# Expert weights of the first chunk: twelve of sixteen rows through DRAM instead of through the PE array, and the router of the other chunks at four steps a period

## The chip, the cores and the metric

The kernel runs on one core of one Trainium2 chip. The metric is the time of one execution on the device, in microseconds; lower is better. Before the change the median of three runs is 518.84 us (518.59 to 519.28).

## The reference, cut to what matters

The program is two layers of several sublayers with residual additions over an input of 16 x 128 tokens of width 128. The change touches only the last sublayer, a mixture of attention projections in which every token weighs 16 experts:

```python
logits = xn @ sn - jax.nn.sigmoid(gates)          # n = 2048 tokens, 16 experts
...
w = jax.nn.softmax(masked, axis=-1)               # the expert weights, (2048, 16)

def moe_proj(p):
    y = jnp.einsum('nc,ech->neh', x, p)
    return jnp.einsum('ne,neh->nh', w, y)
q = moe_proj(q_proj).reshape(b, t, -1)
k = moe_proj(k_proj).reshape(b, t, -1)
v = moe_proj(v_proj).reshape(b, t, -1)
...
o = jnp.einsum('bts,bsh->bth', attn, v).reshape(n, h)
z = jnp.einsum('ne,nh->enh', w, o)
out = jnp.einsum('enh,ehc->nc', z, o_proj)
```

## The kernel before, in words

Everything is written by hand: each of the five engines has its own function with its instructions in order, and semaphores join them. A signal's name stands for a stretch of one of these semaphores (table `LANES`), and `q.wait_ge(name, n)` waits for its n-th signal.

The 2048 tokens lie along the free dimension, in four chunks of 512. Tokens are columns, so weighing the tokens for an expert takes that expert's 512 weights in a row that is the same on all 128 partitions: a *row* of expert weights. The last stage is one loop over `STEPS` = 67 periods k, written in the same shape in `tensor`, `scalar` and `vector`. Period k works on product n = k for the vector and scalar engines and on product n = k - 3 (`LAG`) for the tensor engine; chunk c = n // 16, expert e1 = n % 16:

- VectorE computes `zf` = X5 times the row (L1591, called w(n) below), then the lower half of the split of the product before, l(n) (L1552, `lower`). Then come steps of other work.
- ScalarE rounds `zf` to fp16, the upper half `z_hi` (L988).
- TensorE multiplies both halves by the expert's q and k weights (L673, six matmuls of 512 columns) and its v weights (L681, twelve of 128 columns). This is product P(n). The sums over the experts stay in banks 0, 1 and 2 until P(15), P(31), ..., after which ScalarE (L1010, L1012) and VectorE (L1610) copy q, v and k out.

The buffers `zf` and `ZH` are rings of four, so w, z_hi and l run at most four products ahead of TensorE.

A row reaches all partitions in two ways. For chunk 0, `spread_weights(e1)` (L660) does it in TensorE: a matmul of 32 rows by 512 columns with a selection matrix, into bank 6 or 7. One spread stands in every period up to k = 14. For chunks 1 to 3 the weights are transposed (L733, twelve small transposes, in period `TURN` = 11), copied by ScalarE into 16 partitions (`WTS`, L994, in period `SEND` = 12), written to a DRAM tensor `wd` by one DMA (L1745), and read back by one DMA for each row, which repeats the row on 128 partitions (L1749, 256 KB each), into the places `WR[16]` to `WR[31]` for chunk 1. The vector engine waits for these rows in pairs.

The weights themselves come from the router: 35 dependent small VectorE instructions, once for chunk 0 (before the loop) and once for chunks 1 to 3 together. The latter (`others`) are put into the periods from k = 3 on, five to a period:

```python
if k >= 3:
    for _ in range(5):
        next(others, None)
```

The transposes of period 11 wait for the last of these steps.

Just ahead of the loop TensorE ends the stage before (`mlp_down`, L622), transposes the chunk 0 weights (L652, `turn0`), and ScalarE copies them (L967, `wt16`), adds the bias to the last part of X5 (L945) and squares it (L949); TensorE's logits of chunk 3 (L632, L635) wait for those.

Of the kernel before, what the change touches and what calls it, by code (L numbers as in the profile page):

```python
# [7 lines left out]
F32 = mybir.dt.float32  # L8
# [5 lines left out]
ALU = mybir.AluOpType  # L14
# [36 lines left out]
    (("down", 48), ("weffmm", 4), ("ret_amm", 1), ("fwt", 3), ("wbotmm", 8), ("zmm", 4), ("mlp_down", 16), ("prod_o", 48), ("tile", 4)),  # L51
    (("mean", 4), ("vvmm", 4), ("turn0", 1), ("qkvmm", 12)),
    (("varmm", 4), ("ppmm", 4), ("logits", 4), ("turnw", 3), ("scores", 4)),
    (("x4mm", 4), ("spread", 16), ("xtmm", 4)),
    (("quant_mm", 5), ("pttmm", 4)),
# [4 lines left out]
    (("route_exp", 2), ("theta", 1), ("q_sh", 4), ("sq", 4), ("rt_exp", 2), ("ptt", 4)),  # L60
    (("x_hi", 4), ("wt16", 1), ("wts", 3), ("ot_hi", 3)),

# [49 lines left out]
def program(nc, A, out):  # L112
    with ExitStack() as ctx:
# [70 lines left out]
        def cc(c):  # L184
            return slice(512 * c, 512 * c + 512)

        def bb_(b):
            return slice(128 * b, 128 * b + 128)
# [115 lines left out]
        iota16 = pk1("iota16").rearrange("p (t e) -> p t e", e=16)  # L304
        WTS = RA[0:16, 12288:13824]
        WR = [WEFF[:, 512 * i:512 * i + 512] for i in range(4)] + [QT[:, 512 * i:512 * i + 512] for i in range(4)]
        WR += [STG[:, i // 3, 512 * (i % 3):512 * (i % 3) + 512] for i in range(6)] + [PK0T[:, 512 * i:512 * i + 512] for i in range(3)]
        WR += [WBOT[:, 512 * i:512 * i + 512] for i in range(4)] + [RC[:, 512 * i:512 * i + 512] for i in range(12)]
        wd = nc.dram_tensor("expert_weights", (16, 1536), F32, kind="Internal")
        ID16 = AW16[:, 0, 0:128]  # L310
        W2 = AW16[:, 0, 128:256].rearrange("p (t e) -> p t e", e=32)
# [33 lines left out]
        ZW += [STG[:, i // 3, 512 * (i % 3):512 * (i % 3) + 512] for i in range(6)] + [PK0T[:, 512 * i:512 * i + 512] for i in range(2)]  # L345
        TURN, SEND = 11, 12

# [3 lines left out]
        def tensor(e):  # L351
# [290 lines left out]
            for b in range(4, 18):  # L642
                if b < 16:
                    mlp_up(b)
                mlp_down(b - 2)
                if b in (7, 11, 15):
                    logits(b // 4 - 1)
                if b == 15:
                    q.wait_ge("w2", 2)
                    q.wait_ge("vv", 4)  # L650
                    for i in range(4):
                        t = e.matmul(BK[1][0:32, bb_(i)], W2[:, i, :], ID16, start=True, stop=True)  # L652
                    t.then_inc(S("turn0"), 1)


# [6 lines left out]
            def product(n):  # L662
# [3 lines left out]
                if e1 == 0:  # L666
                    q.wait_ge("router", ROUTER)
                for m in range(2):
# [54 lines left out]
            for k in range(STEPS):  # L723
                if k + 1 < 16:
                    spread_weights(k + 1)
# [42 lines left out]
        def scalar(e):  # L768
# [189 lines left out]
            for b in range(5, 20):  # L958
                if b < 16:
                    su(b)  # L960
                if b in (6, 10, 14, 18):
                    x5((b - 6) // 4)
                if b == 11:
                    router_exp(0, 1)
                if b == 16:
                    q.wait_ge("turn0", 1)
                    e.activation(WT16, BK[1][0:32, :], ACT.Copy).then_inc(S("wt16"), 1)  # L967

            def softmax(c):
# [10 lines left out]
            for k in range(STEPS):  # L980
                if k < NI:
# [6 lines left out]
                    e.activation(ZH[:, r, 0, :], zf[r], ACT.Copy).then_inc(S("z_hi"), 1)  # L988
                if k == 6:
                    router_exp(1, 4)  # L990
# [25 lines left out]
        def vector(e):  # L1016
# [563 lines left out]
            for k in range(STEPS):  # L1580
                if k < NI:
                    c, e1 = k // 16, k % 16
                    if c:
                        q.wait_ge(f"wr{8 * (c % 2) + e1 // 2}", 64 if c == 3 else 32)
                    else:
                        q.wait_ge("spread", e1 + 1)
                    q.wait_ge("x5", c + 1)
                    if k >= 4:
                        q.wait_ge("z_hi", k - 3)
                        q.wait_ge("zlo", k - 3)  # L1590
                    tt(zf[k % 4], X5[:, cc(c)], WR[16 * (c % 2) + e1] if c else BK[6 + e1 % 2][:, :], ALU.mult).then_inc(S("weighed"), 1)  # L1591
                if 0 < k <= NI:
                    lower(k - 1)
                if k >= 3:
                    for _ in range(5):
                        next(others, None)
# [84 lines left out]
        def sync(e):  # L1681
# [60 lines left out]


            q.wait_ge("wts", 3)
            e.dma_start(wd.ap(), WTS).then_inc(S("wst"), 16)  # L1745

            def spread(c, e1):
                row = bass.AP(tensor=wd, offset=e1 * 1536 + 512 * (c - 1), ap=[[0, 128], [1, 512]])
                e.dma_start(WR[16 * (c % 2) + e1], row).then_inc(S(f"wr{8 * (c % 2) + e1 // 2}"), 16)  # L1749

            q.wait_ge("wst", 16)
            q.wait_ge("mlp_down", 16)
            for c in (1, 2):
                for e1 in range(16):
                    spread(c, e1)
            for e1 in range(16):
# [100 lines left out]
```

## Time and profile before

| | |
|---|---|
| median of three runs | 518.84 us (518.59 to 519.28) |
| the profiled execution, its time | 518.41 us |
| the profiled execution, its span in the trace | 516.6 us |
| mean granted TensorE clock | 0.944 |
| busy: TensorE / VectorE / ScalarE / GpSimd | 447.8 / 411.5 / 243.7 / 54.6 us |

The span is the time from the first to the last instruction of the trace; 1.8 us of the execution lie around it. A busy share over the whole span mixes many stages. The stage of the change begins near 312 us and chunk 0 of it ends near 356 us. The rows below are of that stretch; times in them are microseconds from the start of the span.

### The profile page before, as it was taken

What the parts mean: (1) busy time and instruction counts of PE and PEld (TensorE: products, weight loads), DVE (VectorE), ACT (ScalarE), POOL (GpSimd) and SP (SyncE); (2) the same over time, 40 slices, a digit from 0 to 9 for tenths busy, and PEclk for the clock granted to TensorE, in tenths of its full rate; (3) what the DMA queues carried; (4) which work ended last, traced back from release to release, by engine and by line L of the source; (5) the groups of instructions that cost most, each with busy time, mean ns of one, the idle gap of its engine ahead of it and who ended that gap; (6) DMA issues with size and microseconds to landing.
All of it is one profiled execution on the core that took longest, in us unless ns stands there. A gap on an engine that the chain in (4) does not pass through costs nothing.

```text
span 516.6 us, 9115 instructions
## 1 busy us (share of the span) xinstructions
PE 447.8 (87%) x3554; PEld 312.4 (60%) x3554; DVE 411.5 (80%) x850; ACT 243.7 (47%) x419; POOL 54.6 (11%) x69
## 2 busy tenths in 40 slices
PE   2999998999789978500399999999999999999997
PEld 0448998988348843200169986566656565655666
DVE  6989989886597757999853476956798999899786
ACT  5769655563563228895445474334423322332110
POOL 2050000000571004400063000000000000000000
PEclk9999999999899997955599997999999999999999
DMA  7971897930162003403320000019951200000000
GB/s 212 420 305 27 320 354 253 318 139 1 43 189 96 1 1 122 122 0 122 122 83 11 2 1 0 2 21 349 394 202 29 92 6 7 5 11 6 7 5 27
DMA packets 20497, 57.20 MB, mean 111 GB/s; under 512 B 2611, under 2 KB 5046, under 8 KB 20326
## 3 DMA queue, kind: packets, MB, share of 16 engines
q1 hardware_dynamic: 20016, 56.51, 31.3%
q8 instruction: 28, 0.46, 0.4%
q10 hardware_dynamic: 438, 0.11, 0.1%
q14 instruction: 15, 0.12, 0.1%
HBM read 54.41 MB, written 1.15 MB: 108 GB/s over the span
## 4 chain that ended last, share of the span: by engine, by line
PE 66%; DVE 23%; issue 6%; ACT 5%; DMA 0%; DVEq 0%; ACTq 0%
PE bk L673 15%; PE bk L681 8%; PE bk L718 5%; DVE QS L1332 5%; PE bk L369 4%; PE bk L374 4%; PE bk L396 3%; DVE RC L1067 2%; PE bk L614 2%; DVE XT L1564 2%; PE bk L568 2%; DVE RB L1241 2%; PE bk L489 1%; PE bk L498 1%; PE bk L527 1%
## 5 line engine op out<-in xcount | busy, mean ns | idle before, releaser
L673 PE MATMUL bk<-X,RB 128*128 128x512 f16 x384 | 94.6, 383 | 0.0
L988 ACT ACTIVATE X<-RA 128x512 f16<-128x512 f32 x64 | 40.1, 630 | 103.1 <-DVE RA L1591 83.2
L1564 DVE SCALAR_TENSOR_TENSOR XT<-bk,WK,XT 128x128 f32<-128x128 f32 x192 | 67.1, 349 | 6.0 <-PE bk L718 0.8
L673 PEld LDWEIGHTS bk<-X,RB 128*128 128x128 f16 x384 | 36.7, 98 | 43.9 <-issue 4.2
L681 PEld LDWEIGHTS bk<-RB,X 128*128 128x128 f16 x768 | 48.3, 98 | 15.4 <-issue 0.5
L681 PE MATMUL bk<-RB,X 128*128 128x128 f16 x768 | 53.3, 219 | 0.0
L374 PE MATMUL bk<-X,RC 128*128 128x128 f16 x768 | 48.1, 219 | 3.3 <-DVE RC L1067 2.2
L374 PEld LDWEIGHTS bk<-X,RC 128*128 128x128 f16 x768 | 45.1, 98 | 5.7 <-issue 3.8
L1552 DVE TENSOR_TENSOR X<-RA,X 128x512 f16<-128x512 f32 x64 | 43.8, 685 | 1.9 <-ACT X L988 1.9
L1067 DVE SCALAR_TENSOR_TENSOR RC<-RA,RC 128x1024 f16<-128x1024 f32 x32 | 39.1, 1222 | 6.1 <-ACT RC L789 6.1
L824 ACT ACTIVATE WK<-bk 128x512 f32<-128x512 f32 x48 | 28.5, 595 | 25.3 <-PE bk L374 17.6
L718 PE MATMUL bk<-RB,RA 128*128 128x512 f16 x144 | 38.7, 379 | 0.0
L540 PE MATMUL bk<-PK1T,QS 128*128 128x128 f32 x5 | 2.1, 413 | 38.3 <-DVE QS L1335 38.3
L396 PE MATMUL bk<-RB,RA 128*128 128x128 f32 x256 | 34.8, 280 | 0.0
L789 ACT ACTIVATE RC<-RA 128x1024 f16<-128x1024 f32 x32 | 33.6, 1050 | 0.4 <-DMA RA<-in_wx 0.4
L396 PEld LDWEIGHTS bk<-RB,RA 128*128 128x128 f32 x256 | 31.3, 192 | 2.4 <-issue 2.4
L369 PE MATMUL bk<-X,STG 128*128 128x512 f16 x96 | 24.5, 400 | 9.4 <-DVE X L1058 9.4
L1332 DVE TENSOR_REDUCE QS<-RA 128x1 f32<-128x512 f32 (+2 forms) x32 | 29.8, 952 | 2.4 <-ACT RA L898 2.1
L1241 DVE SCALAR_TENSOR_TENSOR RB<-WK,WCOL,bk 128x512 f32<-128x512 f32 x32 | 23.7, 739 | 2.3 <-ACT WK L824 1.8
L540 PEld LDWEIGHTS bk<-PK1T,QS 128*128 128x128 f32 x5 | 0.8, 162 | 39.7 <-DVE QS L1335 39.7
L369 PEld LDWEIGHTS bk<-X,STG 128*128 128x128 f16 x96 | 9.7, 102 | 21.8 <-DVE STG L1063 9.4
L555 PE MATMUL bk<-WK,FW 128*128 128x512 f16 x72 | 18.4, 424 | 2.3 <-DVE WK L1368 2.3
(293 smaller groups left out, 793.4 us busy)
## 6 DMA issues: line engine op xcount, KB each, us to landing
RA<-in_wx SPq DMA_DIRECT2D x32, 768.0 KB, 5.9
RC<-expert_weights SPq DMA_DIRECT2D x22, 256.0 KB, 6.3
X<-in_w SPq DMA_DIRECT2D x8, 512.0 KB, 3.6
RC<-in_w SPq DMA_DIRECT2D x8, 384.0 KB, 4.0
STG<-in_w SPq DMA_DIRECT2D x6, 384.0 KB, 6.8
WBOT<-expert_weights SPq DMA_DIRECT2D x8, 256.0 KB, 6.7
STG<-expert_weights SPq DMA_DIRECT2D x6, 256.0 KB, 8.1
XT<-in_xT SPq DMA_DIRECT2D x4, 256.0 KB, 6.8
```

The source lines that it names most:

```text
L369: t = e.matmul(bank[:, :], W16[:, o:o + 128], X16[:, xp, cc(a)], start=(n == 0), stop=(n == 2))
L374: t = e.matmul(bank[:, bb_(jj)], GU16[:, u % 3, wp, o:o + 128], X16[:, xp, bb_(a)], start=(n == 0), stop=(n == 2))
L396: t = e.matmul(bank[:, bb_(a % 4)], w[:, 1024 + 128 * jj:1152 + 128 * jj], hf[u % 3][:, bb_(jj)], start=(j == 0 and jj == 0), stop=(j == 1 ...
L673: t = e.matmul(BK[m][:, :], P16[:, wp, wo:wo + 128], ZH[:, n % 4, xp, :], start=(e1 == 0 and i == 0), stop=(e1 == 15 and i == 2))
L681: t = e.matmul(BK[2][:, bb_(b)], ZH[:, n % 4, xp, bb_(b)], P16[:, wp, wo:wo + 128], start=(e1 == 0 and b == 0 and i == 0), stop=(e1 == 15 ...
L718: t = e.matmul(bank_o(n)[:, :], OT16[:, xp, bb_(4 * c + b)], P16[:, wp, 6144 + 512 * g:6656 + 512 * g], start=(i == 0), stop=(i == 2))
L988: e.activation(ZH[:, r, 0, :], zf[r], ACT.Copy).then_inc(S("z_hi"), 1)
L1067: stt(GU16[:, u % 3, 1, :], slot(u)[0][:, 0:1024], WS, GU16[:, u % 3, 0, :], ALU.mult, ALU.subtract).then_inc(S("gu_lo"), 1)
L1241: stt(hf[u % 3], ge[u % 3], w, pair(k)[1][:, :], ALU.mult, ALU.mult).then_inc(S("gated"), 1)
L1332: return red(dst, src, X_AX, ALU.max, apply_absolute_value=True)
L1552: tt(ZH[:, n % 4, 1, :], zf[n % 4], ZH[:, n % 4, 0, :], ALU.subtract).then_inc(S("zlo"), 1)
L1564: stt(XT[:, bb_(t_)], bank_o(n)[:, bb_(i)], RW[:, t_, e1:e1 + 1], XT[:, bb_(t_)], ALU.mult, ALU.add).then_inc(S("acc"), 1)
```

## The change

Rows 4 to 15 of chunk 0 no longer go through TensorE. Their weights are transposed in fp32 (`turnw0`, four transposes right behind `turn0`), copied by ScalarE into 16 partitions (`WTS0`), written to a second DRAM tensor `wd0` (32 KB) and read back in twelve DMAs into `WR[4]` to `WR[15]`. Rows 0 to 3 are spread by TensorE as before (`SPREADS` = 4). The router of the other chunks advances four steps in a period instead of five; its transposes move from period 11 to 12, the copies behind them from 12 to 13, and ScalarE's exponential from 6 to 8. The reads of chunk 2's rows 4 to 15 go to the same places and now wait until chunk 0 has used them.

```diff
+        WTS0 = RA[0:16, 6144:6656]
+        wd0 = nc.dram_tensor("expert_weights_first", (16, 512), F32, kind="Internal")
-        TURN, SEND = 11, 12
+        TURN, SEND, SPREADS = 12, 13, 4
...
                     t.then_inc(S("turn0"), 1)
+                    for i in range(4):
+                        t = e.transpose(BK[0][0:16, bb_(i)], RW[:, i, :], pk1("ident"))
+                    t.then_inc(S("turnw0"), 1)
...
             for k in range(STEPS):
-                if k + 1 < 16:
+                if k + 1 < SPREADS:
                     spread_weights(k + 1)
...
                     e.activation(WT16, BK[1][0:32, :], ACT.Copy).then_inc(S("wt16"), 1)
+                    q.wait_ge("turnw0", 1)
+                    e.activation(WTS0, BK[0][0:16, :], ACT.Copy).then_inc(S("wts0"), 1)
...
-                if k == 6:
+                if k == 8:
                     router_exp(1, 4)
...
-                    if c:
-                        q.wait_ge(f"wr{8 * (c % 2) + e1 // 2}", 64 if c == 3 else 32)
+                    if c == 0 and e1 < SPREADS:
+                        q.wait_ge("spread", e1 + 1)
                     else:
-                        q.wait_ge("spread", e1 + 1)
+                        again = c == 3 or c == 2 and e1 >= SPREADS
+                        q.wait_ge(f"wr{8 * (c % 2) + e1 // 2}", 64 if again else 32)
...
                 if k >= 3:
-                    for _ in range(5):
+                    for _ in range(4):
                         next(others, None)
...
+            q.wait_ge("wts0", 1)
+            e.dma_start(wd0.ap(), WTS0).then_inc(S("wst0"), 16)
+            q.wait_ge("wst0", 16)
+            q.wait_ge("mlp_down", 8)
+            for e1 in range(SPREADS, 16):
+                spread(0, e1)
             q.wait_ge("wts", 3)
             e.dma_start(wd.ap(), WTS).then_inc(S("wst"), 16)
...
                 for e1 in range(16):
+                    if c == 2 and e1 >= SPREADS:
+                        q.wait_ge("weighed", e1 + 1)
                     spread(c, e1)
```

TensorE at the head of the stage, before the change. L652 is `turn0`, L622 the end of the stage before, L660 a spread, L632 and L635 the logits, L673 and L681 one product:

```order
210 L652 MATMUL bk<-AW 32x128 x4
211 L622 MATMUL bk<-WK,RC 128x128 x4
212 L660 MATMUL bk<-AW,FW 128x512 x3
213 L632 MATMUL bk<-SM,RA 128x16 x4
214 L635 MATMUL bk<-ONES,RA 128x1 x4
215 L660 MATMUL bk<-AW,FW 128x512 x2
216 L673 MATMUL bk<-X,RB 128x512 x6
217 L681 MATMUL bk<-RB,X 128x128 x12
218 L660 MATMUL bk<-AW,FW 128x512
219 L673 MATMUL bk<-X,RB 128x512 x6
```

The same place with the change (its lines are numbered a little higher: L657 is `turnw0`, L665 a spread):

```order
210 L654 MATMUL bk<-AW 32x128 x4
211 L657 MATMUL bk<-PK1T,WK 16x128 x4
212 L624 MATMUL bk<-WK,RC 128x128 x4
213 L665 MATMUL bk<-AW,FW 128x512 x3
214 L634 MATMUL bk<-SM,RA 128x16 x4
215 L637 MATMUL bk<-ONES,RA 128x1 x4
216 L665 MATMUL bk<-AW,FW 128x512
217 L678 MATMUL bk<-X,RB 128x512 x6
218 L686 MATMUL bk<-RB,X 128x128 x12
219 L678 MATMUL bk<-X,RB 128x512 x6
```

Four transposes stand ahead of the last four `mlp_down` matmuls, one of the two spreads ahead of P(0) is gone, and products follow each other directly.

The steps of the other chunks' router on VectorE with the change, from the period that holds its 24th to 27th step on (L1599 is w, L1559 l, L1537 the router's last step):

```order
397 L1599 TENSOR_TENSOR RA<-RA,STG 128x512
398 L1559 TENSOR_TENSOR X<-RA,X 128x512
399 L1503 TENSOR_TENSOR WK<-WK,SM 128x192
400 L1506 TENSOR_TENSOR WK<-WK,PK1T 128x192
401 L1509 TENSOR_REDUCE SM<-WK 128x12
402 L1512 TENSOR_TENSOR WK<-PK1T,SM 128x192
403 L1599 TENSOR_TENSOR RA<-RA,STG 128x512
404 L1559 TENSOR_TENSOR X<-RA,X 128x512
405 L1515 TENSOR_SCALAR SM<-SM 128x12
...
414 L1537 TENSOR_TENSOR WK<-WK,SM 128x192
415 L1599 TENSOR_TENSOR RA<-RA,STG 128x512
```

The last step now stands behind w(11) and l(10); before it stood behind w(10) and l(9), so one more w and one more l come ahead of it.

SyncE's DMAs at the end of the program with the change (L1760 and L1757 up to PK0T x2 are new):

```order
119 L1749 DMA FW<-in_sel 32x2048
120 L1760 DMA expert_weights_first<-RA 16x512
121 L1757 DMA QT<-expert_weights_first 128x512 x4
122 L1757 DMA STG<-expert_weights_first 128x512 x6
123 L1757 DMA PK0T<-expert_weights_first 128x512 x2
124 L1766 DMA expert_weights<-RA 16x1536
125 L1757 DMA PK0T<-expert_weights 128x512
126 L1757 DMA WBOT<-expert_weights 128x512 x4
```

The thirteen new transfers stand ahead of the write of the other chunks' weights.

## Rows read from the trace of the kernel before

**Rows 1.** The page: TensorE's granted clock in 40 slices, and the chain that ended last.
```profile
PEclk9999999999899997955599997999999999999999
...
PE 66%; DVE 23%; issue 6%; ACT 5%; DMA 0%; DVEq 0%; ACTq 0%
```
**Rows 2.** Timeline, TensorE, two spreads (start us, duration us, engine, line, operation).
```profile
320.91 0.39 PE L660 MATMUL bk<-AW,FW 32*128 32x512 f16 x1
...
323.30 0.38 PE L660 MATMUL bk<-AW,FW 32*128 32x512 f16 x1
```
**Rows 3.** Chain of waits in order of time, products 12, 13 and 16 (start, us).
```profile
348.55 1.29 PE bk L673 x6
...
350.52 1.29 PE bk L673 x6
...
356.41 1.29 PE bk L673 x6
```
**Rows 4.** Timeline, TensorE: head of the stage, and the transposes of period 11.
```profile
310.31 0.40 PE L652 MATMUL bk<-AW 128*32 128x128 f16 x4
310.63 1.16 PE L622 MATMUL bk<-WK,RC 128*128 128x128 f32 x8
...
316.67 1.03 PE L660 MATMUL bk<-AW,FW 32*128 32x512 f16 x2
317.63 2.68 PE L673 MATMUL bk<-X,RB 128*128 128x512 f16 x6
...
337.95 1.48 PE L733 MATMUL bk<-PK1T,WK 128*16 128x128 f32 x12
339.26 1.46 PE L673 MATMUL bk<-X,RB 128*128 128x512 f16 x6
```
**Rows 5.** Timeline, VectorE: w(3), w(4), last router step, w(16), w(18).
```profile
317.31 0.69 DVE L1591 TENSOR_TENSOR RA<-RA,bk 128x512 f32<-128x512 f32 x1 [1.23 <-PE bk L660]
...
319.22 0.68 DVE L1591 TENSOR_TENSOR RA<-RA,bk 128x512 f32<-128x512 f32 x1
...
336.47 0.35 DVE L1530 TENSOR_TENSOR WK<-WK,SM 128x192 f32<-128x192 f32 x1
...
351.11 0.69 DVE L1591 TENSOR_TENSOR RA<-RA,PK0T 128x512 f32<-128x512 f32 x1 [3.30 <-DMA WBOT<-expert_weights]
...
353.52 0.69 DVE L1591 TENSOR_TENSOR RA<-RA,WBOT 128x512 f32<-128x512 f32 x1
```
**Rows 6.** Timeline, ScalarE: wt16, z_hi(12), the three copies, z_hi(16), z_hi(18), q copy.
```profile
310.74 0.59 ACT L967 ACTIVATE AW<-bk 32x512 f16<-32x512 f32 x1 [1.51 <-PE bk L652]
...
341.49 0.63 ACT L988 ACTIVATE X<-RA 128x512 f16<-128x512 f32 x1 [3.06 <-PE bk L681]
342.02 1.52 ACT L994 ACTIVATE RA<-bk 16x512 f32<-16x512 f32 x3
...
351.84 0.63 ACT L988 ACTIVATE X<-RA 128x512 f16<-128x512 f32 x1 [2.56 <-DVE RA L1591]
...
354.54 0.63 ACT L988 ACTIVATE X<-RA 128x512 f16<-128x512 f32 x1 [0.87 <-PE bk L681]
355.13 0.60 ACT L1010 ACTIVATE RA<-bk 128x512 f32<-128x512 f32 x1
```
**Rows 7.** Timeline, SyncE's queue: the write to DRAM and the first row read back.
```profile
343.57 0.31 SPq L1745 DMA_DIRECT2D expert_weights<-RA  x1
346.76 0.34 SPq L1749 DMA_DIRECT2D PK0T<-expert_weights  x1
```
**Rows 8.** Busy time by window: us, PE, PEld, DVE, ACT, POOL, granted clock, DMA.
```profile
313.00:314.00 1.00, 1.00 (x5) 0.79 (x5) 0.43 (x1) 1.00 (x2) 0.00 (x0) 0.64 0.00 0
...
320.00:321.00 1.00, 1.00 (x14) 0.75 (x12) 0.93 (x4) 0.00 (x0) 0.00 (x0) 0.94 0.00 0
...
406.00:408.00 2.00, 0.90 (x12) 0.71 (x9) 1.89 (x6) 1.12 (x2) 0.00 (x0) 1.00 0.12 33
```
**Rows 9.** Waits, VectorE, 330 us to the end (total us, times, longest us).
```profile
DVE RA L1591 <- DMA WBOT<-expert_weights: 3.3, 1, 3.3
```

More of the change, by code:

```diff
@@ L51 @@
     (("down", 48), ("weffmm", 4), ("ret_amm", 1), ("fwt", 3), ("wbotmm", 8), ("zmm", 4), ("mlp_down", 16), ("prod_o", 48), ("tile", 4)),
-    (("mean", 4), ("vvmm", 4), ("turn0", 1), ("qkvmm", 12)),
+    (("mean", 4), ("vvmm", 4), ("turn0", 1), ("turnw0", 1), ("qkvmm", 12)),
     (("varmm", 4), ("ppmm", 4), ("logits", 4), ("turnw", 3), ("scores", 4)),
-    (("x4mm", 4), ("spread", 16), ("xtmm", 4)),
+    (("x4mm", 4), ("spread", 4), ("xtmm", 4)),
     (("quant_mm", 5), ("pttmm", 4)),
@@ L60 @@
     (("route_exp", 2), ("theta", 1), ("q_sh", 4), ("sq", 4), ("rt_exp", 2), ("ptt", 4)),
-    (("x_hi", 4), ("wt16", 1), ("wts", 3), ("ot_hi", 3)),
+    (("x_hi", 4), ("wt16", 1), ("wts0", 1), ("wts", 3), ("ot_hi", 3)),
     (("gated", 48), ("weff", 4), ("sin", 32), ("fw_lo", 3), ("k", 4), ("g", 8), ("x1", 4), ("l_max", 4), ("l_lo", 4),
@@ L666, in product @@
                 if e1 == 0:
-                    q.wait_ge("router", ROUTER)
+                    q.wait_ge("wts0", 1)
                 for m in range(2):
@@ L1590, in vector @@
                         q.wait_ge("zlo", k - 3)
-                    tt(zf[k % 4], X5[:, cc(c)], WR[16 * (c % 2) + e1] if c else BK[6 + e1 % 2][:, :], ALU.mult).then_inc(S("weighed"), 1)
+                    tt(zf[k % 4], X5[:, cc(c)], BK[6 + e1 % 2][:, :] if c == 0 and e1 < SPREADS else WR[16 * (c % 2) + e1], ALU.mult).then_inc(S("weighed"), 1)
                 if 0 < k <= NI:
@@ L1741, in sync, with spread @@
             e.dma_start(SEL, A["sel"]).then_inc(S("sel"), 16)
+            def spread(c, e1):
+                if c:
+                    row = bass.AP(tensor=wd, offset=e1 * 1536 + 512 * (c - 1), ap=[[0, 128], [1, 512]])
+                else:
+                    row = bass.AP(tensor=wd0, offset=e1 * 512, ap=[[0, 128], [1, 512]])
+                e.dma_start(WR[16 * (c % 2) + e1], row).then_inc(S(f"wr{8 * (c % 2) + e1 // 2}"), 16)
+            q.wait_ge("wts0", 1)
+            e.dma_start(wd0.ap(), WTS0).then_inc(S("wst0"), 16)
[3 more added lines that the diff above has]
+                spread(0, e1)
             q.wait_ge("wts", 3)
             e.dma_start(wd.ap(), WTS).then_inc(S("wst"), 16)
-            def spread(c, e1):
-                row = bass.AP(tensor=wd, offset=e1 * 1536 + 512 * (c - 1), ap=[[0, 128], [1, 512]])
-                e.dma_start(WR[16 * (c % 2) + e1], row).then_inc(S(f"wr{8 * (c % 2) + e1 // 2}"), 16)
             q.wait_ge("wst", 16)
```

## The prediction

> **What bounds the kernel now.** I read the page first: the chain that ended last is two thirds TensorE [rows 1]. Then TensorE's timeline through chunk 0, for the distance between two products. While spreads stand between them it is 323.30 - 320.91 = 2.39 us [rows 2]; behind the last spread it is 350.52 - 348.55 = 1.97 us, and P(16) follows P(13) by three times that, 356.41 - 350.52 = 5.89 us [rows 3]. From P(1) to P(16) nothing but spreads and the twelve transposes stands between the products, so TensorE alone sets the pace there. The other engines have room, but how much is the question. The waits of VectorE show one long one, 3.3 us at w(16), for a row that comes through DRAM [rows 9]. It hurts nobody before, as TensorE reaches P(16) only at 356.41 [rows 3], 5.3 us after w(16) at 351.11 [rows 5]. The head of the stage, in the 25th of the 40 slices (a 7 among nines [rows 1]), runs at half clock: 0.64 granted in the first window, 0.94 in the one in which it rises again [rows 8].
>
> **The change part by part.**
>
> *Spreads removed.* One costs 2.39 - 1.97 = 0.42 us. Twelve go; the one ahead of P(0) ran at the low clock, where two took 317.63 - 316.67 = 0.96, so it gives 0.48 [rows 4]. Sum: 0.48 + 11 x 0.42 = **5.1 us** off TensorE's own work.
>
> *Four transposes added.* Twelve of the same kind take 339.26 - 337.95 = 1.31 us, so four take 0.44 [rows 4]. TensorE is what holds the last part of X5 here, so the whole head moves by 0.44: the spread before P(0) starts at 317.11, w(3) at 317.31 + 0.44 = 317.75 [rows 5], P(0) at 317.11 + 0.48 = 317.6, as before. ScalarE's new copy fits in: the three copies of 16 partitions take 1.52, so one 0.5 [rows 6]; it ends at 310.74 + 0.53 + 0.59 = 311.86 by the pitch and the length of its neighbour, and the bias of X5 waits for TensorE until about then anyway. It costs nothing; without that cover it would be 0.5.
>
> *Where TensorE alone would be.* P(0) takes 320.91 - 317.63 = 3.28 at the low clock [rows 2, 4], then P(1) starts at 320.9 and P(8) at 320.9 + 7 x 1.97 = 334.7; it ends at 336.6. Before, the transposes came at 337.95 behind P(7) [rows 4].
>
> *Rows 4 and 5 through DRAM.* Before, from the end of the three copies (342.02 + 1.52 = 343.54) to w(16), which starts with its pair of rows, are 351.11 - 343.54 = 7.57 us [rows 5, 6]; of these 3.2 are the write [rows 7]. With the same delay, rows 4 and 5 are there at 311.86 + 7.57 = 319.43. w(4) wants them at 317.75 + 1.91 - 0.2 = 319.46: w(3) to w(4) was 319.22 - 317.31 = 1.91 [rows 5] with w, l (1.20, below) and four router steps between, and the one step that goes is (1.91 - 1.20) / 4, about 0.2. So they come just in time, with nothing to spare. Later pairs are wanted 4 to 5 us apart by then and are not the risk. Bounds: the write is a third as large, so up to a few tenths earlier, which gives nothing; later passes on one for one.
>
> *The router.* Here is the second price. w(3) to the last step was 336.47 - 317.31 = 19.16 us [rows 5], and VectorE had no wait in it. Now that stretch holds one more w and l. A pair is (353.52 - 351.11) / 2 = 1.20 us [rows 5]. A step at a period's end need not be waited for by w, so one more period end saves a little, 0.1 by my estimate. So the last step starts at 317.75 + 19.16 + 1.20 - 0.1 = 338.0 and ends at 338.4; the transposes start at **338.45**. TensorE stands idle for 338.45 - 336.6 = 1.85 us in front of them, where it had no wait. VectorE needs 338.0 - 317.75 = 20.3 us for the not quite nine periods from 3 to 11, 2.3 a period, while TensorE now needs 1.97: the lead of three periods is used up.
>
> *The rows of chunk 1.* From the transposes everything that follows is a fixed chain. Before: transposes 337.95, one product, z_hi(12) at 341.49, copies until 343.54 [rows 4, 6], w(16) at 351.11. Each of these moves by 338.45 - 337.95 = +0.5, so w(16) starts at 351.6. But TensorE is now due earlier: P(9) at 339.76, P(15) at 339.76 + 6 x 1.97 = 351.6. P(15) needs l(15), which stands behind w(16) on VectorE: ready at 351.6 + 1.3 = 352.9. Second idle time, 1.3 us. P(16) clears bank 0 and needs the q copy. On ScalarE this stands behind z_hi(18), which needs w(18) at 351.6 + 2.41 = 354.0; z_hi follows w by 351.84 - 351.11 = 0.73 and the q copy follows z_hi by 355.13 - 354.54 = 0.59 and takes 0.60 [rows 5, 6]. So the q copy ends at 354.0 + 0.73 + 0.59 + 0.60 = 355.95 and P(16) starts at **356.0**, a third idle time of 1.1. The k copy is ready by then too.
>
> *Sum.* P(16) moves from 356.41 to 356.0: **-0.4 us**. Counted the other way: -5.1 + 0.44 + 1.85 + 1.3 + 1.1 = -0.4. Behind P(16) the period is TensorE's own (with outputs too), and all of it moves along; chunk 2's reads wait for w(4) to w(15), long done. The profiled execution would come from 518.41 to 518.0. That one was 0.43 under the median, so the median goes from 518.84 to **518.4**. What a measurement of this kernel can tell from no change is about 0.2%, 1.04 us; this is inside.
>
> The trace has 7.57 us for write, read and two landings. The Trainium skill, "DMA: Bandwidth & Descriptors", section "Latency and other measured facts", speaks of a DMA fixed cost of about 2 us, mostly the round trip to the memory. By it two transfers in a row would cost some 4 us (an estimate) and w(16) would come up to 3.5 us sooner, no longer in TensorE's way; the trace of before speaks against that with 3.2 us for the write alone [rows 7].
>
> **The rivals.**
>
> *A, the forecast*: the router and the DRAM chain take the place of the spreads. For it: 3.3 us of waiting at w(16) already [rows 9], and VectorE without a gap in periods 3 to 10. Own range 517.6 to 519.2: half a microsecond either way for 7.57 and for the router's end, plus the spread of the runs.
>
> *B, TensorE keeps the pace behind the transposes*, because chunk 1's rows land some 2.5 us sooner than before, on a queue that has just moved chunk 0's. Then P(16) starts at 339.76 + 7 x 1.97 = 353.55: -2.9, a median of 515.9. Against it: the same two transfers in a row, the same size. This is the way that the fixed cost above would lead to.
>
> *C, the clock falls in the new idle time.* Place: the 1.85 us ahead of the transposes. The clock did fall at 313 with TensorE only loosely used [rows 8], and P(0) shows the price: six matmuls of 512 columns took about twice as long [rows 4]. Against it: in the windows with 1.1 us idle later on the clock stayed at 1.00 [rows 8]. At most the transposes and P(9) run at half, +1.31 + 1.97 = +3.3 on the chain of chunk 1's rows, P(16) at 359.3, 521.7; at least nothing. It decides from a delay of 1.45 us on (0.4 to lose, 1.04 to be seen); middle 520.0. [...]
>
> *D, rows 4 and 5 land late.* From 0.4 us late no gain is left, from 1.45 late it is slower by over 0.2%; a microsecond late gives 519.4. For it: nothing to spare. Against it: the write is smaller.
>
> That the change leaves time where it is because the spreads were hidden can't be: 2.39 against 1.97.
>
> **How the numbers follow.** A 0.50, B 0.20, C 0.15, D 0.15. Of A a fifth reaches past -1.04 (0.10) and a little past +1.04 (0.03); B is faster; half of C and half of D are slower, the rest not to be told apart. Faster 0.30, same 0.52, slower 0.18. The range leaves out the far half of B and the upper part of C: 516.2 to 520.0.
>
> **What would show it.** Right: P(n) 1.97 apart from P(1) to P(8); an idle time of 1.5 to 2.2 us on TensorE before the twelve transposes, ended by the router's last step; w(4) with little or no wait for a DMA; idle times of about 1 us each before P(15) and P(16); P(16) between 355.3 and 356.6. Wrong: no idle time before P(15) (B), a granted clock under 1.00 between 336 and 345 us (C), a wait of over 0.4 us at w(4) for a DMA (D). If P(16) starts at 354 or earlier, the chain through DRAM was overrated.

## The result, and the profile after

The changed kernel takes **514.46 us** in the median of four runs (513.73 to 515.09), the kernel before 519.02 on the same chip (four runs, 518.59 to 519.28). The ratio is 0.9916, with an interval of 0.9904 to 0.9928: about 4.4 us faster, where 0.4 us had been forecast and the range ended at 516.2.

| | before | after |
|---|---|---|
| the profiled execution, its time | 518.41 us | 514.77 us |
| its span | 516.6 us | 513.0 us |
| mean granted TensorE clock | 0.944 | 0.950 |
| TensorE / VectorE busy | 447.8 / 411.5 us | 441.2 / 410.0 us |

The page of the changed kernel, TensorE's granted clock and the chain that ended last, against [rows 1]:

```profile
PEclk9999999999899998955599998999999999999999
...
PE 58%; DVE 27%; issue 7%; ACT 6%; DMA 2%; SPq 0%; DVEq 0%; ACTq 0%
```

The clock line has an 8 in two places where [rows 1] has a 7, the slices near 200 us and the head of the stage: less clock was lost in both. TensorE's share of the chain fell from 66% to 58%, and the transfers now hold 2% of it. So part of the way is no longer TensorE's.

**Where the time went.** I looked for one instruction behind which both traces are the same. It is P(16): from its start to the end of the span are 160.3 to 160.4 us in every one of the fourteen traces of this study. In the timeline P(16) starts at 356.25 before (the row below) and at 352.67 now, 3.6 us sooner, as much as the span is shorter (516.6 against 513.0), so the whole difference is ahead of it. ([rows 3] has 356.41 for the same product. That is a row of the chain, which here dates it 0.16 us later than the timeline does; from here on all times are those of the timeline.)

```profile
356.25 1.46 PE L673 MATMUL bk<-X,RB 128*128 128x512 f16 x6
```

TensorE's timeline of the changed kernel, head of the stage (start us, duration us, engine, line, operation, in brackets the idle time before and what ended it), against [rows 4]:

```profile
309.05 0.40 PE L654 MATMUL bk<-AW 128*32 128x128 f16 x4
309.38 0.60 PE L657 MATMUL bk<-PK1T,WK 128*16 128x128 f32 x4
309.82 1.06 PE L624 MATMUL bk<-WK,RC 128*128 128x128 f32 x8
...
312.29 1.06 PE L634 MATMUL bk<-SM,RA 128*128 128x16 f32 x8
313.20 1.03 PE L637 MATMUL bk<-ONES,RA 128*128 128x1 f32 x8
314.17 0.39 PE L665 MATMUL bk<-AW,FW 32*128 32x512 f16 x1
314.49 2.50 PE L678 MATMUL bk<-X,RB 128*128 128x512 f16 x6
...
318.06 1.52 PE L678 MATMUL bk<-X,RB 128*128 128x512 f16 x6
```

The same logits in the kernel before:

```profile
313.21 1.85 PE L632 MATMUL bk<-SM,RA 128*128 128x16 f32 x8
314.89 1.85 PE L635 MATMUL bk<-ONES,RA 128*128 128x1 f32 x8
```

The logits (1.85 + 1.85 before, 1.06 + 1.03 now) run at the full clock. The busy time by window of the changed kernel, with the columns of [rows 8], says the same:

```profile
313.00:314.00 1.00, 1.00 (x12) 1.00 (x11) 0.73 (x2) 0.76 (x2) 0.00 (x0) 1.00 0.31 119
314.00:315.00 1.00, 1.00 (x6) 0.45 (x6) 1.00 (x2) 0.41 (x1) 0.00 (x0) 0.88 0.79 270
315.00:316.00 1.00, 1.00 (x4) 0.38 (x3) 1.00 (x3) 0.43 (x2) 0.00 (x0) 0.50 0.99 348
...
318.00:319.00 1.00, 1.00 (x8) 0.52 (x6) 0.90 (x6) 0.63 (x1) 0.00 (x0) 0.91 1.04 361
```

Half clock from 314.76 to 318.18: 0.24 us of one window (2 x (1 - 0.88)), three whole ones, 0.18 of the last, 3.4 us. Before it was 313.28 to 320.12, 6.8 us [rows 8]. It starts 1.5 us later and is half as long.

TensorE at the transposes, and at P(15) and P(16):

```profile
331.88 1.46 PE L678 MATMUL bk<-X,RB 128*128 128x512 f16 x6
333.18 0.83 PE L686 MATMUL bk<-RB,X 128*128 128x128 f16 x12
335.76 1.48 PE L738 MATMUL bk<-PK1T,WK 128*16 128x128 f32 x12 [1.75 <-DVE WK L1537]
337.07 1.46 PE L678 MATMUL bk<-X,RB 128*128 128x512 f16 x6
...
348.93 1.47 PE L678 MATMUL bk<-X,RB 128*128 128x512 f16 x6
...
352.67 1.45 PE L678 MATMUL bk<-X,RB 128*128 128x512 f16 x6 [1.60 <-ACT RA L1017]
```

The forecast idle time ahead of the transposes is there, 1.75 us, ended by the router's last step. There is none ahead of P(15), and 1.60 us ahead of P(16), ended by the q copy. On the other engines, as in [rows 5] and [rows 6], VectorE with w(4), w(16) and w(18):

```profile
316.77 0.68 DVE L1599 TENSOR_TENSOR RA<-RA,QT 128x512 f32<-128x512 f32 x1
...
347.58 0.69 DVE L1599 TENSOR_TENSOR RA<-RA,PK0T 128x512 f32<-128x512 f32 x1 [4.96 <-DMA WBOT<-expert_weights]
...
350.69 0.69 DVE L1599 TENSOR_TENSOR RA<-RA,WBOT 128x512 f32<-128x512 f32 x1 [0.61 <-DMA WBOT<-expert_weights]
```

ScalarE with the three copies, z_hi(18) and the q copy:

```profile
339.83 1.52 ACT L1001 ACTIVATE RA<-bk 16x512 f32<-16x512 f32 x3
...
351.41 0.63 ACT L995 ACTIVATE X<-RA 128x512 f16<-128x512 f32 x1 [1.28 <-DVE RA L1599]
351.95 0.58 ACT L1017 ACTIVATE RA<-bk 128x512 f32<-128x512 f32 x1
```

And the queue of SyncE, where [rows 7] has 3.19 us between write and first read:

```profile
341.38 0.32 SPq L1766 DMA_DIRECT2D expert_weights<-RA  x1
343.61 0.32 SPq L1757 DMA_DIRECT2D PK0T<-expert_weights  x1
```

w(4) waits for no transfer. w(16) waits 4.96 us for chunk 1's rows, but they are sooner: 347.58 - (339.83 + 1.52) = 6.23 us behind the copies, where 7.57 stood before. The write's share of that is 343.61 - 341.38 = 2.23 us.

### The profile page after: what moved, and what is told of

The parts are those of the page before. It is cut to its first block, busy times and chain, and to the rows that moved or that the text cites. A ratio compares the mean times of both kernels' runs of the same rounds, so it can differ in the third digit from the quotient of the medians.

```text
span 513.0 us, 9108 instructions
## 1 busy us (share of the span) xinstructions
PE 441.2 (86%) x3546; PEld 310.5 (61%) x3546; DVE 410.0 (80%) x850; ACT 243.6 (47%) x420; POOL 54.9 (11%) x69
## 4 chain that ended last, share of the span: by engine, by line
PE 58%; DVE 27%; issue 7%; ACT 6%; DMA 2%; SPq 0%; DVEq 0%; ACTq 0%
PE bk L678 11%; PE bk L686 6%; PE bk L723 5%; DVE QS L1339 5%; PE bk L371 4%; PE bk L376 4%; PE bk L398 3%; PE bk L616 2%; DVE RC L1074 2%; DVE XT L1571 2%; PE bk L570 2%; DVE RB L1248 2%; DVE RA L1599 2%; DVE X L1559 2%; PE bk L491 1%
## 5 line engine op out<-in xcount | busy, mean ns | idle before, releaser
L1559 DVE TENSOR_TENSOR X<-RA,X 128x512 f16<-128x512 f32 x64 | 43.8, 684 | 3.8 <-ACT X L995 3.8
L1673 POOL TENSOR_SCALAR RA<-RA,ROPE 128x128 f32<-128x128 f32 x16 | 9.4, 586 | 101.3 <-ACT RA L857 101.3
```

The lines of the kernel that those rows point to most:

```text
L1559: tt(ZH[:, n % 4, 1, :], zf[n % 4], ZH[:, n % 4, 0, :], ALU.subtract).then_inc(S("zlo"), 1)
```

## The experiments

Twelve measurements; medians, and ratios with their intervals, against runs of the kernel before on the same chip, taken at the same time. The runs fell on two chips, so a difference between two rows is better taken from the ratios than from the medians. "Head" is the time from `turn0` to P(1), "half clock" a stretch in which the granted clock is 0.5, the level of 1.2 GHz. Two such stretches are the same in all fourteen traces and are left out: 3.4 us long near 137 us, and 41 us long from about 216 us on. Two change in length, one near 195 to 200 us, far ahead of the change, and one at the head; the kernel with five steps has one more. The last column is P(16) in the profiled run.

| kernel | median us | ratio | head us | half clock near 200 / at the head, us | P(16) |
|---|---|---|---|---|---|
| before, again | 518.83 | 1.0002 [0.9992, 1.0011] | 10.92 | 6.8 / 6.8 | 356.58 |
| before + four transposes | 516.61 | 0.9963 [0.9950, 0.9977] | 9.90 | 3.4 / 3.4 | 354.13 |
| before + a gap instead | 519.89 | 1.0016 [1.0005, 1.0027] | 12.15 | 6.8 / 10.2 | 358.25 |
| before + four steps | 519.29 | 1.0009 [1.0001, 1.0018] | 10.92 | 6.8 / 6.8 | 357.60 |
| before + late start | 520.39 | 1.0025 [1.0014, 1.0036] | 10.92 | 6.8 / 6.8 | 358.6 |
| before + early write | 518.83 | 0.9997 [0.9986, 1.0007] | 12.06 | 3.4 / 10.2 | 356.62 |
| after, all rows spread | 517.12 | 0.9965 [0.9951, 0.9979] | 9.78 | 6.8 / 3.4 | 355.96 |
| after, again | 514.64 | 0.9925 [0.9911, 0.9939] | 8.93 | 3.4 / 3.4 | 352.53 |
| after, five steps | 516.49 | 0.9962 [0.9948, 0.9977] | 9.01 | 3.4 / 3.4 | 353.38 |
| after, copies first | 513.64 | 0.9903 [0.9887, 0.9918] | 8.42 | 6.8 / 3.4 | 351.51 |
| ... and periods 13, 14 | 513.43 | 0.9899 [0.9885, 0.9913] | 9.01 | 3.4 / 3.4 | 350.29 |
| ... and periods 13, 13 | **511.49** | 0.9867 [0.9853, 0.9881] | 8.39 | 6.8 / 3.4 | 349.27 |

### Both kernels again

No edit to either. Before:

> The kernel before, unchanged. The profiled run of before had TensorE at the low clock for 58.0 us in all (1 - 0.944, doubled, times 516.6), the changed kernel for 51.4 us. Theory 'the clock's stretches belong to the kernel': every run here shows a mean clock of 0.943 to 0.945 and the time is 518.5 to 519.4. Rival 'the stretches fall by chance': mean clocks of single runs vary between 0.943 and 0.951 and the times with them by 2 us or more.

After:

> The changed kernel, unchanged. 'Belong to the kernel': mean clock 0.949 to 0.951 in all runs, 514.0 to 515.1. 'By chance': some runs at 0.944 with 516 us or more.

518.83 and 514.64 us: the gain holds in a second measurement. Neither expectation fits quite. The single runs of before spread from 517.84 to 519.81 us, with low time of 57.8 to 61.1 us in all; four of the five runs of the changed kernel have 51.3 us, one has 54.5. So a part of the low time varies from run to run, but the two kernels don't overlap in it. (Low time is 2 x (1 - mean clock) x span.) The new trace of the changed kernel has the same 1.75 us ahead of the transposes and only 0.90 us ahead of P(16):

```profile
336.34 1.48 PE L738 MATMUL bk<-PK1T,WK 128*16 128x128 f32 x12 [1.75 <-DVE WK L1537]
...
352.53 1.46 PE L678 MATMUL bk<-X,RB 128*128 128x512 f16 x6 [0.90 <-ACT RA L1017]
```

There w(18) had no wait for its rows, where the first trace had 0.61 us. From transposes to P(16) are 352.53 - 336.34 = 16.19 us, against the 17.55 forecast and 16.91 in the first trace.

### Four transposes alone, and a gap in their place

The change has two parts at the head: four more transposes, and one spread less. The first question is whether the transposes keep the clock up. Before, with the transposes and nobody to read them (added work, nothing else):

```diff
                     t.then_inc(S("turn0"), 1)
+                    for i in range(4):
+                        t = e.transpose(BK[0][0:16, bb_(i)], RW[:, i, :], pk1("ident"))
+                    t.then_inc(S("turnw0"), 1)
```

> The kernel before with only the four fp32 transposes behind turn0 added; nobody reads them. From the start of turn0 to the start of P(1) it was 10.9 us in three traces of before and 12.1 in one, with the clock low there for 6.8 or 10.2 us; 9.8 with the transposes and all spreads. Theory 'the four transposes keep the clock up through the logits': the clock is low for 3.4 us less or more here, turn0 to P(1) takes 9.7 to 10.0, the sum of low stretches falls from 57.9 to 54.6 or below in all runs, 517.3 to 518.0. Rival 'they only cost their own 0.44 us; the clock rose for another reason (copy, missing spreads)': 11.3, low for 57.9, 519.3.

And before with TensorE held back at that place by a small VectorE instruction. It costs 0.27 us there (0.59 from `turn0` to L622, where before had 0.32), the transposes 0.45:

```diff
                     t.then_inc(S("turn0"), 1)
+                    q.wait_ge("gap", 1)
...
+            q.wait_ge("turn0", 1)
+            e.memset(SM[:, 39, 0:4], 0.0).then_inc(S("gap"), 1)
```

> The kernel before with a wait of TensorE in place of the four transposes: it waits for a tiny memset on VectorE that itself waits for turn0, some 0.4 us without work. Theory 'it is the work of the transposes': the clock stays low for 57.8 or more, 519.2 to 519.6. Rival 'it is the shift by 0.4 us': as with the transposes, 54.6 and 518.

The transposes alone give 0.9963 x, 1.9 us faster, although they are pure extra work. The gap gives 1.0016 x, 0.8 us slower, a little more than expected. TensorE and the clock, first with the transposes:

```profile
309.53 0.61 PE L655 MATMUL bk<-PK1T,WK 128*16 128x128 f32 x4
...
312.45 1.06 PE L632 MATMUL bk<-SM,RA 128*128 128x16 f32 x8
313.36 1.03 PE L635 MATMUL bk<-ONES,RA 128*128 128x1 f32 x8
```

then with the gap:

```profile
311.11 1.16 PE L622 MATMUL bk<-WK,RC 128*128 128x128 f32 x8 [0.19 <-DVE SM L1552]
...
313.71 1.89 PE L632 MATMUL bk<-SM,RA 128*128 128x16 f32 x8
```

and the windows of the kernel with the gap:

```profile
313.00:314.00 1.00, 0.64 (x3) 0.38 (x3) 0.90 (x2) 0.97 (x3) 0.00 (x0) 0.80 0.00 0
314.00:315.00 1.00, 1.00 (x6) 1.00 (x6) 0.34 (x1) 1.00 (x3) 0.00 (x0) 0.50 0.00 0
...
323.00:324.00 1.00, 1.00 (x4) 0.40 (x3) 1.00 (x3) 0.00 (x0) 0.00 (x0) 0.58 0.00 0
```

So it is not a delay as such that helps: with the gap the low stretch lasts until 323.8, with the transposes it is 3.4 us (314.9 to 318.4) and the logits are done before it. The delays differ by 0.2 us (0.27 and 0.45), and a gap of the full 0.45 us was not tried, so that it is the work and not its length is likely, but not shown to the end. The single runs agree with the traces: the six with the transposes have 51.4 to 54.7 us of low time, nine of the eleven with the gap 61.2 or more and two 57.8, and none of 61 runs of before, measured beside the experiments, has under 57.8. And over the whole table the split is clean: in all eight traces of kernels with the four transposes (the first of the changed kernel counted) the head has 3.4 us at half clock, in all six without them 6.8 or 10.2, whatever the stretch near 200 was.

### Four steps to a period alone, and every row spread

Before, with the router's part of the change only:

```diff
-        TURN, SEND = 11, 12
+        TURN, SEND = 12, 13
...
-                if k == 6:
+                if k == 8:
...
-                    for _ in range(5):
+                    for _ in range(4):
```

> The kernel before with only the router edit: four steps a period, transposes in 12, copies in 13, exponential in 8. TensorE gets to the transposes behind P(8) with its spreads, later than the router ends, so no idle time there. Theory 'chunk 1's rows then hold P(16)': the copies end 2.4 us later, w(16) too, the q copy ends 0.5 to 1.4 us after P(16) was due: 519.4 to 520.3, an idle time ahead of P(16). Rival 'there is slack enough': 518.9.

After, with all sixteen rows spread by TensorE again (transposes and steps stay):

```diff
-        TURN, SEND, SPREADS = 12, 13, 4
+        TURN, SEND, SPREADS = 12, 13, 16
```

> The changed kernel with all 16 rows spread by TensorE again; the four transposes, their copy, the 32 KB write and the slower router stay. Against the kernel before: theory of the forecast, head +0.4 and the later router through chunk 1's rows about +1, so 519.5 to 520.5, and against the changed kernel the twelve spreads show with 5 to 6 us. Rival 'most of the gain is the clock': if the changed kernel's higher clock comes from its head (transposes), it stays here too and the time is 516.5 to 518.

Four steps alone are 0.5 us slower by the ratio (1.0009), just clear of no change. The wait that was expected ahead of P(16) is there, 0.55 us for the q copy:

```profile
357.60 1.46 PE L673 MATMUL bk<-X,RB 128*128 128x512 f16 x6 [0.55 <-ACT RA L1010]
```

With the transposes too it is 0.9965, -1.8 us, where the two parts alone would give -1.9 + 0.5 = -1.4; this fits the rival 'most of the gain is the clock'. The twelve spreads less are worth 517.12 - 514.64 = **2.5 us** by the medians, both from one chip, and 2.1 by the ratios, not the 5 to 6 of the expectation: about half of the 5.1 by which they shorten TensorE's own work. Each of these parts is uncertain by some 0.7 us, so that they add up (-1.9 + 0.5 - 2.1 = -3.5, measured -3.9) tells no more than that no large part is missing.

### Five steps to a period in the changed kernel

```diff
-        TURN, SEND, SPREADS = 12, 13, 4
+        TURN, SEND, SPREADS = 11, 12, 4
...
-                if k == 8:
+                if k == 6:
...
-                    for _ in range(4):
+                    for _ in range(5):
```

> The changed kernel with only its router edit undone: five steps a period, transposes in period 11, copies in 12, exponential in 6. Theory 'the router's end holds TensorE': the idle time before the twelve transposes stays over 1 us (they now come one product sooner, but the router ends only 1.1 us sooner), chunk 1's rows land 1.1 us sooner, P(16) starts about 1 us sooner, 513.3 to 513.8. Rival 'router pace does not matter' (TensorE makes up for it by P(16)): within 0.4 us of the changed kernel.

516.49 us, 1.85 slower than four steps. Both expectations failed, since neither had the clock in it. TensorE and its clock there:

```profile
334.67 2.17 PE L738 MATMUL bk<-PK1T,WK 128*16 128x128 f32 x12 [2.59 <-DVE WK L1537]
336.63 2.49 PE L678 MATMUL bk<-X,RB 128*128 128x512 f16 x6
```

```profile
335.00:336.00 1.00, 1.00 (x9) 0.69 (x7) 1.00 (x3) 0.63 (x1) 0.00 (x0) 0.65 0.00 0
336.00:337.00 1.00, 1.00 (x5) 0.57 (x4) 1.00 (x3) 0.00 (x0) 0.00 (x0) 0.50 0.00 0
...
338.00:339.00 1.00, 1.00 (x5) 0.35 (x4) 0.00 (x0) 0.00 (x0) 0.00 (x0) 0.65 0.00 0
```

This is rival C at work. The idle time is 2.59 us instead of 1.75, and behind it the clock is at half from 335.3 to 338.7: the transposes take 2.17 instead of 1.48, the first matmuls of the product behind them 2.49 instead of 1.46. In the changed kernel the window from 335 to 337 was granted 1.00. This trace is of the fastest of the six runs (515.49 us) and has 54.5 us of low time; three others have 57.7 to 58.7, so part of the price in the median may be a further low stretch, which no trace shows. So the pace of four steps costs 0.5 us where spreads give the router time, and spares 1.85 us where they don't.

### The copies for chunk 1's rows ahead of z_hi

In the changed kernel the three copies stand behind z_hi(13) on ScalarE, which waits for the ring to come free. They are moved ahead of it:

```diff
             for k in range(STEPS):
+                if k == SEND:
+                    for c in (1, 2, 3):
+                        q.wait_ge("turnw", c)
+                        e.activation(WTS[:, 512 * c - 512:512 * c], BK[2 + c][0:16, :], ACT.Copy).then_inc(S("wts"), 1)
                 if k < NI:
...
-                if k == SEND:
...
```

> The changed kernel with ScalarE's three copies of the transposed weights ahead of z_hi(13) in period 13 instead of behind it. Theory 'chunk 1's rows through DRAM hold P(16)': the copies end 3.0 us after the transposes start instead of 5.6, w(16) comes 2.6 us sooner, the idle time ahead of P(16) (1.6 and 0.9 us in two traces) goes, P(16) starts 15.1 us after the transposes instead of 16.2 to 16.9: 1.1 to 1.8 us faster than the changed kernel, 512.8 to 513.6. Rival 'P(16) waits for the q copy for another reason': w(16) moves, P(16) does not, 514.6.

513.64 us, 1.0 better. The copies end 2.6 us behind the start of the transposes (339.08 against 336.44) instead of 5.6, w(16) starts at 345.34, and P(16) at 351.51 has no idle time before it, 15.07 us behind the start of the transposes, as expected. So it was this chain that had held P(16) in the changed kernel.

### The transposes one period later

With the copies first, the transposes and the copies move one period later, so that the router has time:

```diff
-        TURN, SEND, SPREADS = 12, 13, 4
+        TURN, SEND, SPREADS = 13, 14, 4
```

> The same with the transposes one period later (period 13, copies at the head of 14), behind P(9). Theory: TensorE's 1.75 us of idle time ahead of the transposes is filled with P(9), since the router's end, not the transposes' place, sets their start; they start as before and P(16) follows 13.1 us behind them: 2.0 us faster than with the transposes in 12, 510.8 to 511.6. Rival 'the freed time comes back as a wait for chunk 1's rows ahead of P(15) or P(16)': 512.5 or more.

and then with the copies a period earlier:

```diff
-        TURN, SEND, SPREADS = 12, 13, 4
+        TURN, SEND, SPREADS = 13, 13, 4
```

> The changed kernel with the transposes in period 13 behind P(9) and ScalarE's three copies at the head of period 13, ahead of z_hi(13), which was late in the run with copies in 14 (they began 2.05 us after the transposes started, not 1.12). Theory: copies end 2.7 us after the transposes start, w(16) near 8.9 us after it, the q copy 13.2 us after it, where P(16) is due at 13.1: idle times ahead of P(15) and P(16) 0.2 us together instead of 1.3, 1.0 to 1.2 us under that run, 512.2 to 512.5. Rival 'another wait takes its place': 513.4.

With 13 and 14 the 1.75 us ahead of the transposes are gone, and most of it is back later:

```profile
347.25 1.47 PE L678 MATMUL bk<-X,RB 128*128 128x512 f16 x6 [0.36 <-DVE X L1559]
...
350.29 1.46 PE L678 MATMUL bk<-X,RB 128*128 128x512 f16 x6 [0.90 <-ACT RA L1017]
```

513.43 us, which can't be told from the 513.64 of periods 12 and 13. The expected 510.8 to 511.6 was missed; the rival, that the freed time comes back as a wait, is what happened. With 13 and 13 both waits are gone:

```profile
336.12 1.47 PE L738 MATMUL bk<-PK1T,WK 128*16 128x128 f32 x12
...
347.26 1.46 PE L678 MATMUL bk<-X,RB 128*128 128x512 f16 x6
348.55 0.83 PE L686 MATMUL bk<-RB,X 128*128 128x128 f16 x12
349.27 1.46 PE L678 MATMUL bk<-X,RB 128*128 128x512 f16 x6
```

From P(1) to P(16) TensorE has no wait left: 349.27 - 317.76 = 31.51 us, which is fifteen products of 1.97 (29.55), the transposes (1.31) and 0.65 us for the end of the head's half clock, in which P(1) begins. **511.49 us**, the fastest kernel here, even a little under the expected 512.2 to 512.5; 3.0 us under the change and 7 under before. So the waits that ate half of the removed spreads were one chain from the router's end to the q copy, and it can be taken out of TensorE's way.

### Does the start of the stage, or the queue's state, matter?

Two attempts at the rest. Before, started later by three VectorE instructions that nothing needs (TensorE's first matmul is at 11.00 us instead of 9.44):

```diff
+            for i in range(3):
+                e.memset(WEFF[:, cc(i)], 0.0).then_inc(S("late"), 1)
+            q.wait_ge("late", 3)
             sh_lo(0)
```

> The kernel before with three memsets of unused memory ahead of the first split on VectorE, which start TensorE about 1 us later (the trace will tell). Theory 'how long the clock stays low at a place depends on when in the run the work resumes, by chance of the build': the low stretches near 200 and 313 us change from 6.8 us each to 3.4 for one or both, and the time changes by +1 less 0.9 for each. Rival 'the stretches belong to the code around them': both stay at 6.8 and the time is 1 us longer.

Before, with a small write to DRAM early, as the changed kernel has one, to see if a used queue makes the later write faster:

```diff
+            q.wait_ge("sel", 16)
+            q.wait_ge("wt16", 1)
+            e.dma_start(spare.ap(), SEL[0:16, 0:1024]).then_inc(S("spare"), 16)
+            q.wait_ge("spare", 16)
             q.wait_ge("wts", 3)
```

> The kernel before with one more write of 32 KB to a spare DRAM tensor at the place of the changed kernel's first write; nothing reads it. The write of the other chunks' weights took 3.2 us from issue to the next DMA in two traces of before, 2.2 to 2.5 in four traces with the earlier write. Theory 'an earlier write makes the later one faster': 2.2 to 2.5 here. Rival 'it is another property of the build or of the place': 3.2. The time stays at 518.9 either way, since w(16) is not in TensorE's way there.

The late start costs about what it is long, 1.3 us by the ratio for 1.6 us, and the stretches are still 6.8 and 6.8. This one shift of the whole program changed nothing in them. The early write changes nothing in the time: 518.83 us. The later write took 2.98 us, which is neither the 2.2 to 2.5 of the one expectation nor the 3.2 of the other; a write ahead of it is in any case not enough to make it as quick as in the changed kernel. Its trace is worth more for its clock: 3.4 us near 200, and then 10.2 us at the head (311.62 to 321.86), so P(16) is where it was, at 356.62 (356.58 in the new trace of before).

## Why the prediction was wrong, and where it was right

In the profiled runs P(16) was forecast at 356.0 and came at 352.67. (The forecast set its 356.0 against the chain's 356.41 of [rows 3]; against the timeline's 356.25 the step that it foresaw is 0.25 us and not 0.4, which changes nothing below.) The 3.3 us come from four places, in the order of the text:

**The start.** `turn0` at 309.05 against 310.31: **-1.26**. The code ahead is the same. The stretch of half clock near 200 us was 3.4 us in this run and 6.8 in the profiled run of before. Both lengths occur with the old head and with the new one (the table), so this part belongs to the run and not to the change's own code. The prediction had no term for it and could have none from one trace. With the old head the gain doesn't stay, though: in the one such trace with 3.4 us near 200 (the early write) the head had 10.2 instead of 6.8, and P(16) came no sooner. The low time of the changed kernel's nine runs was about 51.3 or 54.5 us, while in none of the 61 runs of before beside the experiments was it under 57.8. So by these runs the earlier start is kept only with the new head. That link is seen, not explained.

**"The whole head moves by 0.44 ... P(0) at 317.6, as before."** This step failed, and it is the largest of the change's own. `turn0` to P(1) was forecast at 10.6 us and took 9.01, **-1.6**. The four transposes were priced as 0.44 us of cost, at a clock taken over from before. They do push the logits back by 0.34 us (309.05 to 312.29 = 3.24; before 310.31 to 313.21 = 2.90), but logits and the spread behind them then take 314.49 - 312.29 = 2.20 us instead of 317.63 - 313.21 = 4.42 with two spreads. P(0), now wholly at half clock, gives 0.27 back (318.06 - 314.49 = 3.57, forecast 3.3). Alone they make before 1.9 us faster; a gap at the same place makes it slower. The prediction had looked at the clock only as a thing that might fall in new idle time (rival C), never as one that added work might hold up. It also read [rows 8] wrong there: "TensorE only loosely used" it says of the window at 313 us, in which the row has TensorE busy 1.00. By that row the busy share alone doesn't tell whether the clock holds, so there was no ground for taking the head's low stretch over unchanged.

**The router.** Right. The idle time ahead of the transposes was to be 1.85 us and is 1.75, ended by the router's last step; P(1) to the transposes was to take 17.55 and takes 17.70 (+0.15). The products are 1.97 us apart. This is what a spread less is worth as long as nobody waits: 0.42 each.

**"w(16) at 351.6 (7.57 us after the copies)."** A term mis-sized. It measured 6.23 and 6.20 us in the two traces of the changed kernel: -1.35. With this value in the forecast's own chain, the transposes to P(16) come to 17.55 - 1.35 = 16.20, and the second trace has 16.19. In the first the rows of w(18) were late as well, 16.91 (**-0.64**). The wait ahead of P(15), forecast 1.3, went with it: w(16) at 347.58 plus the pair of w and l, 1.3, is 348.88, and P(15) started at 348.93 with TensorE there 0.07 earlier. The 7.57 was one profile's, and the largest: the six other traces of before and its variants have 6.16 to 7.23.

Sum: -1.26 - 1.6 + 0.15 - 0.64 = -3.3. The medians have the rest (519.0 to 514.5, where the profiled runs have 518.4 to 514.8), since the profiled run of before was 0.6 us under that median and the changed kernel's 0.3 us over its own.

**Rows 4 and 5** were in time, as forecast: w(4) had no wait for a transfer. The write of 32 KB took 1.6 us from its issue to the first read, half of the larger one before. Rival D is not seen.

**Rival B** came true by a half: rows sooner, by 1.35 instead of 2.5 us, so TensorE kept pace at P(15) and not at P(16). Its reason, a queue that has just moved chunk 0's rows, is not borne out: with five steps the queue has moved them too and the write takes 2.5 us, and before with four steps, without them, it takes 2.2. The changed kernel's write of 2.2 us is near the fixed cost of about 2 us that the Trainium skill gives in "DMA: Bandwidth & Descriptors", section "Latency and other measured facts". The 3.2 us of before, which the prediction had held against it, is not the usual length. For both transfers together the estimate of 4 us was too short, with 6.23 us measured up to w(16). **Rival C** did not happen here, with idle times of 1.75 and 1.60 us, and did with five steps, with 2.59 us; its price, with the idle time itself, was 1.85 us in the median. The Trainium skill, "TensorE: Matmul & The Clock Gate", section "HAM oscillation — how this bites in real kernels", describes a kernel in which TensorE waits some 3 to 5 us for a transfer between bursts of matmuls, and each burst starts cold. The idle times here are all shorter than those; the clock fell behind the one of 2.59 us.

Not settled: why the write of the weights of chunks 1 to 3 takes 2.2 us (2.22 to 2.23) in seven traces, and 2.5 to 3.2 in the other seven. Each of the slow ones shows one packet of 0.02 MB on the queue for instructions between the write and the first read. Six of the quick ones show none, but the seventh (copies first) has one in the last half microsecond of its write, and is no slower. So a link with such a fetch is possible at most, and nothing here tests it.

## What to carry to other kernels

Before pricing an edit next to a stretch of low clock, ask what it does to the work just ahead of the fall, in both directions, and don't take a busy share of 1.00 for a sign that the clock holds: 0.45 us of otherwise useless matmuls bought 1.9 us here, and a gap of 0.27 us lost 0.8. When work is taken off the engine that sets the pace, follow each producer to its own due time and move it in its engine's order at once; some 3 of the 5.1 us came only with the copies moved ahead of a waiting instruction and the transposes one period on. And a duration that carries a forecast should come from more than one profile: two of the misses (1.26 and 1.35 us) lie within what the traces of before and its small variants show (a `turn0` at 309.3, 6.2 to 7.2 us).

## What the runs showed of the hardware

- At two places of the program a stretch of half clock came as 3.4, 6.8 or 10.2 us in fourteen traces, and 3.4 us less of it were worth about 1 us: of the six runs with the four transposes alone, three had 51.4 to 51.5 us of low time and took 516.15 us in the mean, three had 54.6 to 54.7 and took 517.18. One run of the changed kernel had 54.5 instead of 51.3, at 515.66 us against the median of 514.64.
- TensorE counted as busy throughout does not keep the clock: at 313 it was busy 1.00 of the window in both kernels, and was granted 0.64 before [rows 8] and 1.00 after; with the four transposes alone (their busy time 1.00 too) it was also 1.00.
- Idle times of 1.75 and 1.60 us among products cost no clock; behind one of 2.59 us, in the one trace that has it, the clock was at half for 3.4 us.
- A write of 96 KB to DRAM took 2.2 us from its issue to that of the read behind it in seven traces, and 2.5 to 3.2 us in seven.
